# State space stage of a fused block: B held twice so that keys by queries is one product per batch, and another order of work in the first and the last group of heads

## The chip, the cores and the metric

The kernel runs on one core of a Trainium2 chip. The metric is the device time of one execution in microseconds (us); lower is better. The core's engines run side by side, each through its own list of instructions in a fixed order, and wait for one another on semaphores: TensorE (PE), which multiplies matrices, VectorE (DVE), ScalarE (ACT), GpSimd (POOL), and SyncE (SP), which here starts the transfers.

## What is computed

A block of three layers on x, 8 batches of 64 tokens with 512 features: cross attention over 1601 keys with 32 heads, then a Mamba-2 layer, then a routed mixture of rank 16 experts. The change is in the second. Cut to what matters:

```python
proj = x @ in_proj_w.T                       # gate | x, B, C | dt
xBC = silu(conv_bias + causal 4-tap conv of the x, B, C part)
dt = softplus(dt + dt_bias);  dA = exp(-dt * exp(A_log))
# 64 heads of 64 channels, 8 groups of 8 heads; a group shares B and C (128 each)
state = state * dA_t + (dt_t * x_t) outer B_t         # for each token t
y_t   = state @ C_t + D * x_t
y     = rmsnorm over a group's 512 channels * norm_weight * silu(gate)
out   = y @ out_proj_w.T
```

A scan over 64 tokens is done as a quadratic form: `y = (mask * exp(decays) * (B . C)) @ (dt * x)` for each batch and head.

## The kernel before

The stage `state_space_and_experts` loops over the 8 groups `g` of heads (0 to 7; `L` is 7), and within a group over 4 tiles `t` of 128 tokens (two batches each). A group takes ten **input chunks** of 128 columns of the input projection: `n` from 0 to 3 are the gates, 4 to 9 are four of x, then B, then C. `input_chunk(g, n)` is 12 f16 products of 128x128 by 128x512 into one of three banks `pI`, so that each chunk waits until the one three places before has been read. Its readers are, for a gate, `gates` on ACT, and for the rest `first_tap` (ACT), `taps` (three instructions on DVE) and `finish_conv` (ACT, which applies silu).

For a tile then come, on PE: `turn_x` (four transposes of x), `keys_by_queries` (B times C, f32), `decay` (sums of logarithms, from ramps that POOL makes with `ramp`), `outputs` (16 small products), `squares` (a sum for the norm) and `out_tile` (the output projection of one tile, again 12 products). On ACT `exponentials` reads what `decay` made, and `square` and `high` make squares and the f16 high half of y. On DVE `times_dt` multiplies the turned x by dt, `causal` masks keys by queries, `masked` joins them to the exponentials, `skip_added` and `gated` finish y, `accumulate` adds an output tile to x1, and `split_A`, `split_B` and `split_C` make f16 low halves of weights that arrived in f32 (A: the columns of x, B, C; B: the gates'; C: the output's). POOL has `ramp`, `join_squares`, `low` (the f16 low half of y) and `power` (the norm's root). After tile `t` of the last group the experts' work follows: `moments`, `normed`, `turn_normed`, `logits`, `route`, `turn_weighted`, `expert_out`, `add_experts`.

The order of all these calls is written out by hand, one list for each engine: `body` for groups 0 to 6, which interleaves a group with what is left of the one before, and `last` for group 7. In `body` a call `on(f, g, lag, ...)` is the call for group `g - lag`, and is left out where there is none. Tiles that share a PSUM bank are guarded by counts: `turn_x` waits until every `decay` begun so far has been read by its exponential,

```python
def turn_x(g, t):
    wait(pe, silu, CONV * g + GCH)
    wait(pe, dx, TT * g + t)
    wait(pe, e_ok, begun["d"])
```

and `out_tile` waits, as long as it uses the one bank `pO`, for the `accumulate` of the tile before. Ahead of the loop DVE computes dt for all groups in a chain of small instructions (L2005 to L2022). The first group's weights are loaded and split by `SsmStart`, during the attention's output projection.

## Time and profile before

| | |
|---|---|
| three runs | 2360.22, 2360.7, 2362.95 us (median 2360.7) |
| the profiled execution | 2363.03 us, span 2360.7 us |
| attention and its projections | to about 1938 us of the span |
| state space stage and experts | from about 1938 us to the end |
| mean granted clock of PE | 0.989 |

All durations below come from the one profiled execution. A row of a timeline gives start, duration, engine, line, operation, output from inputs, shape and count, and in brackets how long the engine had been idle and what released it. A product in f32 leaves two records, and records overlap, so that the time which a call takes on PE is read from its start to the start of the next. A granted clock of 1.00 is 2.4 GHz, 0.50 is 1.2 GHz.

### The profile page before, as it was taken

To read this page: it belongs to the slowest core of one execution; us is meant where nothing else is said; L and a number is where in the kernel's file an instruction comes from. 1 tells how busy PE (TensorE), PEld (TensorE's weight loads), DVE (VectorE), ACT (ScalarE), POOL (GpSimd) and SP (SyncE) were. 2 spreads that over 40 slices of the span, in tenths; PEclk is the share of its full clock that TensorE was granted. 3 is DMA by queue.
4 is the path that set the end of the run, shared out by engine and by line. 5 is a ranking of instruction groups with operands and counts; after the bars stand their busy time and mean duration, and the time that the engine had idled before them with its cause. 6 is when DMAs were issued, how large, how long until landed. Compare 5 with 4: busy or idle time off the path is not lost. (4 is left out here: it accounts for less than half of the span.)

```text
span 2360.7 us, 46502 instructions
## 1 busy us (share of the span) xinstructions
PE 2291.3 (97%) x19276; PEld 1651.5 (70%) x19276; DVE 1915.2 (81%) x2596; ACT 1295.4 (55%) x2085; POOL 1567.5 (66%) x1056
## 2 busy tenths in 40 slices
PE   7999999999999999999999999999999788999998
PEld 4567787788777887778877887778877344445544
DVE  6858888888888888888888888888879756888877
ACT  7845455554555455554555545554455336666664
POOL 0138888888888888888878888888878202334432
PEclk9999999999999999999999999999999998999999
DMA  8420000000001010010001000000002541212210
GB/s 287 125 53 28 26 26 26 29 26 26 26 26 32 19 34 26 18 28 26 26 26 32 27 26 26 26 28 10 11 26 63 166 164 48 98 64 81 90 46 19
DMA packets 101166, 117.54 MB, mean 50 GB/s; under 512 B 8286, under 2 KB 70878, under 8 KB 100958
## 3 DMA queue, kind: packets, MB, share of 16 engines
q1 hardware_dynamic: 98942, 107.25, 14.4%
q0 software_dynamic: 2016, 7.34, 1.2%
q8 instruction: 153, 2.51, 0.4%
q14 instruction: 55, 0.45, 0.1%
HBM read 96.74 MB, written 17.83 MB: 49 GB/s over the span
## 5 line engine op out<-in xcount | busy, mean ns | idle before, releaser
L174 POOL TENSOR_TENSOR p_l<-S,p_h 128x1792 f16<-128x1792 f32 x126 | 422.7, 3355 | 211.7 <-ACT p_h L469 211.7
L577 DVE SCALAR_TENSOR_TENSOR S<-pS,rk,mask 128x256 f32<-128x256 f32 x832 | 355.4, 477 | 133.0 <-PE pS L257 92.4
L257 PE MATMUL p_acc<-w_h,ctx_h 128*128 128x256 f16 (+1 forms) x1664 | 454.3, 273 | 0.0
L257 PE MATMUL p_acc<-w_l,ctx_h 128*128 128x256 f16 (+1 forms) x1664 | 454.3, 273 | 0.0
L257 PE MATMUL p_acc<-w_h,ctx_l 128*128 128x256 f16 (+1 forms) x1664 | 454.3, 273 | 0.0
L587 DVE TENSOR_REDUCE mx<-S 128x256 f32<-128x3328 f32 x64 | 382.7, 5980 | 2.2
L257 PE MATMUL p_acc<-ctx_h,w_h 128*128 128x400 f16 (+1 forms) x1024 | 341.3, 333 | 3.0 <-PEq L820 3.0
L257 PE MATMUL p_acc<-ctx_l,w_h 128*128 128x400 f16 (+1 forms) x1024 | 341.2, 333 | 0.0
L257 PE MATMUL p_acc<-ctx_h,w_l 128*128 128x400 f16 (+1 forms) x1024 | 340.4, 332 | 0.0
L451 ACT ACTIVATE v_h<-p_acc 128x512 f16<-128x512 f32 (+1 forms) x224 | 126.8, 566 | 379.5 <-PE p_acc L257 379.5
L679 POOL TENSOR_TENSOR sq_l<-sq_f,sq_h 128x400 f16<-128x400 f32 (+1 forms) x256 | 243.0, 949 | 69.9 <-ACT sq_h L443 69.9
L599 DVE TENSOR_TENSOR S<-S,pO 128x1792 f32<-128x1792 f32 (+1 forms) x128 | 240.2, 1878 | 6.8 <-PE pO L327 6.8
L257 PE MATMUL pO<-p_h,v_h 128*128 128x256 f16 x832 | 226.8, 273 | 3.1 <-DVE p_l L174 3.1
L257 PE MATMUL pS<-qh,k_h 128*128 128x256 f16 x832 | 226.5, 272 | 1.0 <-DVE S L577 1.0
L257 PE MATMUL pS<-qh,k_l 128*128 128x256 f16 x832 | 226.8, 273 | 0.0
L257 PE MATMUL pO<-p_h,v_l 128*128 128x256 f16 x832 | 226.8, 273 | 0.0
L257 PE MATMUL pO<-p_l,v_h 128*128 128x256 f16 x832 | 226.8, 273 | 0.0
L257 PE MATMUL pS<-ql,k_h 128*128 128x256 f16 x832 | 226.7, 272 | 0.0
L462 ACT ACTIVATE S<-S,lnb 128x1792 f32<-128x1792 f32 (+1 forms) x128 | 215.5, 1684 | 17.5 <-DVE S L599 17.5
L182 POOL TENSOR_TENSOR S<-S 128x1536 f32<-128x1536 f32 x63 | 216.8, 3441 | 0.1
L439 ACT ACTIVATE k_h<-p_acc 128x400 f16<-128x400 f32 (+1 forms) x256 | 129.8, 507 | 147.1 <-PE p_acc L257 145.1
L469 ACT ACTIVATE p_h<-S 128x1792 f16<-128x1792 f32 (+1 forms) x128 | 203.6, 1591 | 0.3
(286 smaller groups left out, 5229.9 us busy)
## 6 DMA issues: line engine op xcount, KB each, us to landing
ctx_p<-ctxT_dram SPq DMA_DIRECT2D x42, 458.0 KB, 3.5
s_wst<-winG_dram SPq DMA_DIRECT2D x8, 1536.0 KB, 6.4
q_wst<-wqT_dram SPq DMA_DIRECT2D x8, 1024.0 KB, 6.5
o_scratch<-o_st SPq DMA_DIRECT2D x32, 256.0 KB, 2.4
s_wst<-winG_dram SPq DMA_DIRECT2D x8, 1024.0 KB, 5.3
m_wost<-woutG_dram SPq DMA_DIRECT2D x8, 1024.0 KB, 5.3
qh<-q_hi_scratch SPq DMA_DIRECT2D x64, 64.0 KB, 1.9
ql<-q_lo_scratch SPq DMA_DIRECT2D x64, 64.0 KB, 2.0
```

The source lines that it names most:

```text
L174: eng.tensor_tensor(p_l[:, s % 2, t0:t1, :], S[:, s % 2, t0:t1, :], p_h[:, s % 2, t0:t1, :], ALU.subtract).then_inc(pl_ok, 1)
L182: eng.tensor_tensor(T[:, 0:6, :], T[:, 0:6, :], T[:, 6:12, :], ALU.add).then_inc(sum_ok, 1)
L257: mm = pe.matmul(out, x, y, start=first and j == 0, stop=final and j == 2)
L439: act.activation(k_h[:, head % 2, c0:c0 + w], bank[:, 0:w], ACT.Copy, scale=S_KV / (S_CTX * S_W))
L451: act.activation(v_h[0:m, job % 2, 2 * f:2 * f + tiles, :], pF[at % 3][0:m, 0:256 * tiles].rearrange("p (t c) -> p t c", c=256), ACT.Copy, ...
L462: act.activation(S[:, s % 2, t0:t1, :], S[:, s % 2, t0:t1, :], ACT.Exp, bias=lnb[:, 0:1]).then_inc(ph_ok, 1)
L469: act.activation(p_h[:, s % 2, t0:t1, :], S[:, s % 2, t0:t1, :], ACT.Copy).then_inc(ph_ok, 1)
L577: ins = dve.scalar_tensor_tensor(out=S[:, s % 2, t, :].rearrange("p (r q) -> p r q", r=REP), in0=bank[:, t % 2, :].rearrange("p (r q) -> p ...
L587: dve.tensor_reduce(mx[:, :], S[:, s % 2, :, :].rearrange("p t q -> p q t"), AX.X, ALU.max).then_inc(mx_ok, 1)
L599: dve.tensor_tensor(v, v, pO[s % 2][:, 1, :].unsqueeze(1).to_broadcast([P, t1 - t0, QC]), ALU.subtract).then_inc(sub_ok, 1)
L679: pool.tensor_tensor(sq_l[:, c0:c0 + w], sq_f[:, c0:c0 + w], sq_h[:, c0:c0 + w], ALU.subtract).then_inc(sql_ok, 1)
```

## The change

- `keys_by_queries` had, per batch of a tile, two products of 64 keys by 64 queries with the same operands, one for each half of the partitions of `pCB`. B is now held twice in `bq` (per batch, its 64 tokens and the same again), and one product of 128 by 64 writes both halves. `finish_conv` for B writes both copies, in one activation that reads its input twice.
- Groups 0 and 7 take the chunks in the order 4 to 9, 0 to 3. `place(g, n)` is a chunk's place among all, `order(g)` a group's order; banks and waits follow from them. The other groups keep 0 to 9.
- In group 0 all ten chunks, and ACT's work on them, are written as one run at the head of `body`, with `decay(0, 0)` behind them. `step_sizes` and the exponential of that `decay` come after the gates.
- `SsmStart` loads and splits A ahead of B. `split_B` of the next group waits for the place of the last gate chunk.
- `last` is written anew on PE, ACT, DVE and POOL.

```diff
     def load(self, sp, w):
+        sp.dma_start(self.wst[:, :, 0:CW], w[:, 0:CW].rearrange("(k p) c -> p k c", p=P)).then_inc(self.wA_in, 16)
         sp.dma_start(self.wst[:, :, CW:], w[:, CW:].rearrange("(k p) c -> p k c", p=P)).then_inc(self.wB_in, 16)
-        sp.dma_start(self.wst[:, :, 0:CW], w[:, 0:CW].rearrange("(k p) c -> p k c", p=P)).then_inc(self.wA_in, 16)
...
-        bc = sb("m_bc", [P, 2, ND])
+
+        bq = sb("m_bq", [P, BATCH, 2, TOK])
+        cq = sb("m_cq", [P, ND])
...
+        def order(g):
+
+            return (*range(GCH, NIN), *range(GCH)) if g in (0, L) else tuple(range(NIN))
+
+        def place(g, n):
+
+            return NIN * g + order(g).index(n)
...
                 if n == 0:
                     wait(pe, wB_lo, g + 1)
-                    wait(pe, conv, CONV * g)
                 if n == GCH:
                     wait(pe, wA_lo, g + 1)
-                if n >= 3 + GCH:
-                    wait(pe, conv, CONV * g + n - GCH - 2)
-                elif n >= 3:
-                    wait(pe, gat, GCH * g + n - 2)
+                m = place(g, n)
+                if m >= 3:
+
+                    og = (m - 3) // NIN
+                    on_ = order(og)[(m - 3) % NIN]
+                    if on_ < GCH:
+                        wait(pe, gat, GCH * og + on_ + 1)
+                    else:
+                        wait(pe, conv, CONV * og + on_ - GCH + 1)
...
                     cols = slice(t * P + 64 * b, t * P + 64 * b + 64)
-                    for e in range(2):
-                        mm = pe.matmul(pCB[64 * e:64 * e + 64, 64 * b:64 * b + 64], bc[:, 0, cols], bc[:, 1, cols], start=True, stop=True)
+                    mm = pe.matmul(pCB[:, 64 * b:64 * b + 64], bq[:, 2 * t + b, :, :].rearrange("p e q -> p (e q)"), cq[:, cols], start=True, stop=True)
                 mm.then_inc(cb, 1)
...
                 wait(act, wB_in, 16 * (g + 1))
-                wait(act, ip, NIN * (g - 1) + GCH)
+                wait(act, ip, place(g - 1, GCH - 1) + 1)
...
+                elif j == GCH:
+                    act.activation(bq[:, :, :, :], cv[:, j % 2, :].rearrange("p (b q) -> p b q", b=BATCH).unsqueeze(2).to_broadcast([P, BATCH, 2, TOK]),
+                                   ACT.Silu).then_inc(silu, 1)
                 else:
-                    act.activation(bc[:, j - GCH, :], cv[:, j % 2, :], ACT.Silu).then_inc(silu, 1)
+                    act.activation(cq[:, :], cv[:, j % 2, :], ACT.Silu).then_inc(silu, 1)
```

What the new lists do is seen from the instructions. First ACT in group 0, before (`m_gate` gates, `m_Ec` exponentials, `m_cv` first taps, `m_xq` silu of x, `m_dtq` step sizes):

```order
L1801 ACT_TABLE_LOAD
L1801 ACTIVATE m_gate<-m_b 128x512 x4
L1824 ACT_TABLE_LOAD
L1824 ACTIVATE m_Ec<-m_ab 128x512
L1808 ACTIVATE m_cv<-m_b,m_par 128x512 x2
L1816 ACT_TABLE_LOAD
L1816 ACTIVATE m_xq<-m_cv 128x8x64
L1808 ACTIVATE m_cv<-m_b,m_par 128x512
L1816 ACTIVATE m_xq<-m_cv 128x8x64
L1772 ACTIVATE m_dtq<-m_dt 64x128 x4
```

and the same group's end in the change (`m_bq` silu of B, twice as wide, `m_cq` of C, `s_wh` the next group's weights):

```order
L1846 ACTIVATE m_cv<-m_b,m_par 128x512
L1856 ACTIVATE m_bq<-m_cv 128x1024
L1859 ACTIVATE m_cq<-m_cv 128x512
L1839 ACTIVATE m_gate<-m_b 128x512 x4
L1810 ACTIVATE m_dtq<-m_dt 64x128 x4
L1865 ACT_TABLE_LOAD
L1865 ACTIVATE m_Ec<-m_ab 128x512
L1826 ACTIVATE s_wh<-s_wst 128x4x512
```

The first exponential has moved from behind the gates at the head to behind the gates at the end and the step sizes.

Second, DVE at the head of the last turn, before (`x` is `accumulate`, `m_yt` `skip_added`, `m_E` `masked`, `s_wl` the splits, B's with 512 and A's with 768 columns):

```order
L1985 SCALAR_TENSOR_TENSOR s_wl<-s_wst,s_wh 128x4x512
L2095 SCALAR_TENSOR_TENSOR x<-m_b,m_rs,x 128x512
L2068 SCALAR_TENSOR_TENSOR m_yt<-m_xq,m_par,m_cd 128x128 x4
L2059 TENSOR_TENSOR m_E<-m_Ec,m_cbm 128x512
L2078 TENSOR_TENSOR m_y<-m_yt,m_gate 128x512
L2051 TENSOR_TENSOR m_cbm<-m_cd,m_upto 128x128
L2059 TENSOR_TENSOR m_E<-m_Ec,m_cbm 128x512
L2068 SCALAR_TENSOR_TENSOR m_yt<-m_xq,m_par,m_cd 128x128 x4
L2078 TENSOR_TENSOR m_y<-m_yt,m_gate 128x512
L2095 SCALAR_TENSOR_TENSOR x<-m_b,m_rs,x 128x512
L2051 TENSOR_TENSOR m_cbm<-m_cd,m_upto 128x128
L1978 SCALAR_TENSOR_TENSOR s_wl<-s_wst,s_wh 128x4x768
```

and in the change:

```order
L2061 SCALAR_TENSOR_TENSOR s_wl<-s_wst,s_wh 128x4x512
L2135 TENSOR_TENSOR m_E<-m_Ec,m_cbm 128x512
L2171 SCALAR_TENSOR_TENSOR x<-m_b,m_rs,x 128x512
L2144 SCALAR_TENSOR_TENSOR m_yt<-m_xq,m_par,m_cd 128x128 x4
L2054 SCALAR_TENSOR_TENSOR s_wl<-s_wst,s_wh 128x4x768
L2127 TENSOR_TENSOR m_cbm<-m_cd,m_upto 128x128
L2171 SCALAR_TENSOR_TENSOR x<-m_b,m_rs,x 128x512
```

A's split has moved ahead of the second `accumulate`, that of tile 2 of group 5.

Third, PE late in the last turn, around the first `out_tile` of group 7, before (`L738` are chunks and output tiles, `L1610` keys by queries, `L1568` `decay`, `L1618` `squares`, `L1585` `outputs`, `L1599` `turn_x`):

```order
L1610 MATMUL m_cd<-m_bc 64x64 x4
L1568 MATMUL m_ab<-m_R,s_after 64x256 x4
L1610 MATMUL m_cd<-m_bc 64x64 x4
L1618 MATMUL m_cd<-s_ones,m_sqb 128x1
L1610 MATMUL m_cd<-m_bc 64x64 x4
L1585 MATMUL m_cd<-m_E,m_dtx 64x64 x16
L1568 MATMUL m_ab<-m_R,s_after 64x256 x4
L1599 MATMUL m_ab<-s_ident,m_xq 128x128 x4
```

and the same place in the change, with the last gate chunk ahead of it (12 rows of L738 each where the dots are, a chunk and then the output tile):

```order
L1624 MATMUL m_cd<-m_cq,m_bq 128x64 x2
...
L1632 MATMUL m_cd<-s_ones,m_sqb 128x1
L1624 MATMUL m_cd<-m_cq,m_bq 128x64 x2
L1583 MATMUL m_ab<-m_R,s_after 64x256 x4
L1600 MATMUL m_cd<-m_E,m_dtx 64x64 x32
...
L1624 MATMUL m_cd<-m_cq,m_bq 128x64 x2
L1614 MATMUL m_ab<-s_ident,m_xq 128x128 x4
```

Two tiles' `outputs` stand together now, and the keys of the last tile have moved behind the output tile. The whole new list of PE from there on: `out_tile(7,0)`, keys and `turn_x` of tile 3, `squares(7,1)`, `out_tile(7,1)`, `outputs(7,3)`, `turn_normed(0)`, `squares(7,2)`, `out_tile(7,2)`, `squares(7,3)`, `turn_normed(1)`, `logits(0)`, `logits(1)`, `out_tile(7,3)`. At its head the last turn has on PE: `out_tile(5,3)`, `decay(6,3)`, `outputs(6,2)`, `turn_x(6,3)`, chunk 4, keys of (6,3), `decay(7,0)`, chunk 5, `decay(7,1)`. Chunks 0 to 3 stand behind `out_tile(6,1)`, `turn_x(7,1)`, `turn_x(7,2)` and keys of (7,1).

## Rows read from the trace of the kernel before

**Rows 1.** Page, part 1: busy time of each engine and its share.

```profile
PE 2291.3 (97%) x19276; PEld 1651.5 (70%) x19276; DVE 1915.2 (81%) x2596; ACT 1295.4 (55%) x2085; POOL 1567.5 (66%) x1056
```

**Rows 2.** Busy time by stretch, middle: stretch, length, PE, PEld, DVE, ACT, POOL, PEclk, DMA.

```profile
2060.00:2120.00 60.00, 59.08 (x454) 30.17 (x452) 50.75 (x79) 40.44 (x53) 23.17 (x22) 1.00 0.22 74
```

**Rows 3.** Chain that ended last, two groups' first taps of C: start, us, what.

```profile
2071.18 0.79 ACT m_cv L1808
...
2117.83 0.79 ACT m_cv L1808
```

**Rows 4.** Busy time by stretch, both ends, columns as in rows 2.

```profile
1979.19:1993.05 13.86, 7.96 (x118) 5.51 (x116) 10.78 (x18) 10.44 (x11) 3.89 (x3) 0.69 0.24 76
2272.17:2343.98 71.81, 64.97 (x543) 33.41 (x537) 54.50 (x100) 35.99 (x54) 31.63 (x34) 0.95 0.07 24
2343.98:2360.70 16.72, 11.93 (x62) 6.82 (x59) 11.23 (x34) 3.38 (x9) 0.32 (x1) 0.98 0.17 63
```

**Rows 5.** Timeline of PE, middle: squares (L1618), keys (L1610), a chunk's first product.

```profile
2070.98 0.50 PE L1618 MATMUL m_cd<-s_ones,m_sqb 128*128 128x1 f32 x4
...
2097.59 0.28 PE L1618 MATMUL m_cd<-s_ones,m_sqb 128*128 128x1 f32 x2
2097.80 0.45 PE L1610 MATMUL m_cd<-m_bc 128*64 128x64 f32 x8
2098.18 0.39 PE L738 MATMUL m_b<-m_th,s_wh 128*128 128x512 f16 x1
...
2252.22 0.28 PE L1618 MATMUL m_cd<-s_ones,m_sqb 128*128 128x1 f32 x2
2252.36 0.38 PE L738 MATMUL m_b<-m_th,s_wh 128*128 128x512 f16 x1
```

**Rows 6.** Timeline of PE, from group 0 to group 1: keys, decay, next group's first chunk.

```profile
1983.19 0.45 PE L1610 MATMUL m_cd<-m_bc 128*64 128x64 f32 x8 [3.40 <-ACT m_bc L1818]
...
1985.11 1.13 PE L1568 MATMUL m_ab<-m_R,s_after 64*64 64x256 f32 x8 [0.42 <-DVE m_dtx L2044]
...
1993.05 0.61 PE L738 MATMUL m_b<-m_th,s_wh 128*128 128x512 f16 x1
```

**Rows 7.** Timeline of DVE, start of the stage: x1, end of the dt chain, first taps.

```profile
1935.51 2.49 DVE L1228 SCALAR_TENSOR_TENSOR x<-p_acc,p_x 128x512 f32<-128x512 f32 x4 [10.57 <-PE p_acc L738]
...
1960.67 0.29 DVE L2022 TENSOR_SCALAR m_dt<-m_dt 128x256 f32<-128x256 f32 x1
1967.25 2.27 DVE L2034 SCALAR_TENSOR_TENSOR m_cv<-m_b,m_par,m_cv 128x504 f32<-128x504 f32 x3 [6.29 <-ACT m_cv L1808]
```

**Rows 8.** Timeline of ACT, group 0: step sizes, weight split, table load, exponential.

```profile
1973.04 1.29 ACT L1772 ACTIVATE m_dtq<-m_dt 64x128 f32<-64x128 f32 x4
...
1983.05 1.89 ACT L1788 ACTIVATE s_wh<-s_wst 128x2048 f16<-128x2048 f32 x1
1984.96 1.28 ACT L1824 ACT_TABLE_LOAD   x1
1986.30 0.60 ACT L1824 ACTIVATE m_Ec<-m_ab 128x512 f32<-128x512 f32 x1
```

**Rows 9.** Busy time by stretch, after group 0's chunks, columns as in rows 2.

```profile
1985.00:1987.00 2.00, 1.14 (x9) 0.37 (x10) 2.00 (x3) 1.95 (x3) 0.66 (x1) 0.50 0.00 0
```

**Rows 10.** Timeline of PE, last turn: `turn_x(7,0)` and `decay(7,3)` after waits.

```profile
2309.86 0.63 PE L1599 MATMUL m_ab<-s_ident,m_xq 128*128 128x128 f32 x4 [2.16 <-ACT m_Ec L1824]
...
2325.44 0.90 PE L1568 MATMUL m_ab<-m_R,s_after 64*64 64x256 f32 x8 [1.39 <-POOL m_R L1444]
```

**Rows 11.** Chain that ended last, first and last `out_tile` of group 7.

```profile
2328.21 4.80 PE m_b L738 x12
...
2344.14 2.59 PE m_b L738 x12
```

**Rows 12.** Timeline of DVE, A's split in group 1 and in group 7.

```profile
1998.86 4.20 DVE L1978 SCALAR_TENSOR_TENSOR s_wl<-s_wst,s_wh 128x3072 f16<-128x3072 f32 x1
...
2275.63 3.34 DVE L1978 SCALAR_TENSOR_TENSOR s_wl<-s_wst,s_wh 128x3072 f16<-128x3072 f32 x1
```

More of the change, by code:

```diff
@@ L1552, in out_tile @@
                     wait(pe, conv, CONV * (g + 1))
+                    wait(pe, gat, GCH * (g + 1))
                 for j in range(GCH):
@@ L1702, in last @@
+                decay(g, 0)
+                input_chunk(g, 5)
+                decay(g, 1)
+                squares(g - 1, 0)
+                input_chunk(g, 6)
+                squares(g - 1, 1)
                 outputs(g - 1, 3)
-                input_chunk(g, 5)
+                input_chunk(g, 7)
                 out_tile(g - 1, 1 - par, 0)
-                input_chunk(g, 6)
                 squares(g - 1, 2)
-                input_chunk(g, 7)
                 input_chunk(g, 8)
+                squares(g - 1, 3)
@@ L1709, in last @@
                 input_chunk(g, 9)
-                squares(g - 1, 3)
-                decay(g, 0)
+                out_tile(g - 1, 1 - par, 1)
+                input_chunk(g, 0)
                 turn_x(g, 0)
-                out_tile(g - 1, 1 - par, 1)
+                out_tile(g - 1, 1 - par, 2)
+                turn_x(g, 1)
+                input_chunk(g, 1)
                 keys_by_queries(g, 0)
-                turn_x(g, 1)
-                out_tile(g - 1, 1 - par, 2)
-                decay(g, 1)
+                out_tile(g - 1, 1 - par, 3)
@@ L1718, in last @@
                 outputs(g, 0)
-                out_tile(g - 1, 1 - par, 3)
+                turn_x(g, 2)
+                input_chunk(g, 2)
+                decay(g, 2)
                 keys_by_queries(g, 1)
-                decay(g, 2)
+                input_chunk(g, 3)
+                squares(g, 0)
                 keys_by_queries(g, 2)
-                squares(g, 0)
+                decay(g, 3)
+                outputs(g, 1)
+                outputs(g, 2)
+                out_tile(g, par, 0, out_bank[0])
@@ L1724, in last @@
                 keys_by_queries(g, 3)
-                outputs(g, 1)
-                decay(g, 3)
-                turn_x(g, 2)
-                out_tile(g, par, 0, out_bank[0])
                 turn_x(g, 3)
-                outputs(g, 2)
+                squares(g, 1)
                 out_tile(g, par, 1, out_bank[1])
                 outputs(g, 3)
-                squares(g, 1)
+                turn_normed(0)
+                squares(g, 2)
                 out_tile(g, par, 2, out_bank[2])
-                squares(g, 2)
@@ L1797, in gates @@
             def gates(g, par, n):
-                wait(act, ip, NIN * g + n + 1)
+                wait(act, ip, place(g, n) + 1)
                 if n == 0:
                     wait(act, yg, TT * (g - 1))
-                act.activation(gate[:, par, n, :], pI[n % 3][:, :], ACT.Silu, scale=1.0 / (S_H * S_W)).then_inc(gat, 1)
+                act.activation(gate[:, par, n, :], pI[place(g, n) % 3][:, :], ACT.Silu, scale=1.0 / (S_H * S_W)).then_inc(gat, 1)
             def first_tap(g, j):
-                wait(act, ip, NIN * g + GCH + j + 1)
+                wait(act, ip, place(g, GCH + j) + 1)
                 wait(act, silu, CONV * g + j - 1)
@@ L2169, in last @@
                 split_B(g)
+                masked(g - 1, 1)
                 accumulate(g - 2, 1)
                 skip_added(g - 1, 0)
-                masked(g - 1, 1)
+                split_A(g)
+                causal(g - 1, 2)
+                accumulate(g - 2, 2)
+                times_dt(g - 1, 2)
+                skip_added(g - 1, 1)
+                masked(g - 1, 2)
                 gated(g - 1, 1 - par, 0)
-                causal(g - 1, 2)
-                masked(g - 1, 2)
-                skip_added(g - 1, 1)
@@ L2177, in last @@
                 gated(g - 1, 1 - par, 1)
-                accumulate(g - 2, 2)
+                skip_added(g - 1, 2)
+                times_dt(g - 1, 3)
+                accumulate(g - 2, 3)
                 causal(g - 1, 3)
-                split_A(g)
-                times_dt(g - 1, 2)
-                skip_added(g - 1, 2)
+                masked(g - 1, 3)
+                taps(g, 0)
                 split_C(g - 1, 1 - par)
-                masked(g - 1, 3)
-                times_dt(g - 1, 3)
+                skip_added(g - 1, 3)
@@ L2186, in last @@
+                taps(g, 1)
                 gated(g - 1, 1 - par, 2)
-                accumulate(g - 2, 3)
-                taps(g, 0)
-                skip_added(g - 1, 3)
+                taps(g, 2)
+                mean_square(g - 1)
                 gated(g - 1, 1 - par, 3)
-                taps(g, 1)
-                taps(g, 2)
+                accumulate(g - 1, 0)
                 taps(g, 3)
                 taps(g, 4)
-                mean_square(g - 1)
-                accumulate(g - 1, 0)
+                accumulate(g - 1, 1)
@@ L2219, in last @@
                 gated(g, par, 2)
-                times_dt(g, 3)
-                accumulate(g, 0)
-                skip_added(g, 3)
-                moments(0)
-                tile_mean_square(g, 1)
-                gated(g, par, 3)
+                accumulate(g, 0)
+                moments(0)
+                causal(g, 3)
+                masked(g, 3)
+                tile_mean_square(g, 1)
+                times_dt(g, 3)
                 normed(0)
                 accumulate(g, 1)
+                skip_added(g, 3)
@@ L2241, in last @@
                 route(2)
+                route(3)
                 add_experts(1)
-                route(3)
                 add_experts(2)
```

266 lines of the change are left out of this document (157 added, 109 removed).

## The prediction

> **What bounds the kernel now.** I read the page's head first, then busy time by stretch, the chain that ended last, and the timelines of the two places that the change touches. TensorE (PE) is busy for 97% of the span [rows 1]. The change leaves attention alone, so what counts is the state space stage, from 1940 us on. Its middle is bound by PE: in a 60 us stretch PE is busy 59.08 us at full clock, the vector engine (DVE) 50.75 [rows 2], and a group of heads comes every 46.65 us (2117.83 less 2071.18 [rows 3]). Its two ends are not. The first group has 13.86 us between its last input chunk and the next group's first, in which PE works 7.96 us at a mean clock of 0.69. In the last turn PE is idle 6.84 of the 71.81 us up to its last `out_tile`, and then 4.79 of 16.72 [rows 4]. So the middle can gain only by less PE work, the ends by shorter chains of waits.
>
> **Keys by queries, 32 calls.** Four products of 64x64 become two of 128x64, with the batch's B, held twice, as the 128 stationary columns. A call takes 0.38 us now, start to start (2097.80 to 2098.18 [rows 5]), for eight records. Half the records does not mean half the time. The row to go by is the one for squares: f32 as well, with 128 stationary columns and one moving column, and two more of its records cost 0.22 us (four are busy 0.50, two 0.28), so 0.11 each though almost nothing streams: the weights take that. Four such records make 0.44. On the other side, a call now also delays its neighbour: squares, keys and the next chunk take 0.59 (2097.59 to 2098.18), squares alone 0.14 (2252.22 to 2252.36), so keys really cost 0.45. Thus 0.45 now against 0.44 then: nothing. After a wait the first weights cannot be hidden, which costs up to 0.1 once per group; a call followed by a transpose may gain that. I take 0. Bounds: if a merged record kept the pace of one of today's records, a call would take 0.19, and 0.19 x 3 x 8 groups = 4.6 us go; the fourth call of a group stands before a `decay` that waits anyway. If each call grew by 0.06 (0.44 against 0.38), 1.4 us come.
>
> The Trainium skill, "TensorEngine Tiling (Array Packing)", sections Key Properties and Performance Considerations, speaks against the merger: products in different column tiles run in parallel, so merging two of them saves no streaming, though it saves the drain at a mode switch. The same section has the opposite rule too: a product with one moving column takes as long as one with 60, about 60 cycles, which here would make the call cheap. "TensorE: Matmul & The Clock Gate", section LDWEIGHTS, counts by stationary columns, P/1.2 ns: 107 ns for 128, and 0.43 for a call. The 0.11 of [rows 5] agrees with that.
>
> The copy of B makes one activation per group write 1024 elements per partition, not 512. The weight split writes 2048 in 1.89 us and the exponential 512 in 0.60 [rows 8], so, in line between them, about 1.03, 0.43 more. It runs while DVE does the 2.27 us of taps for C, which C's own activation awaits [rows 7, 8]: no cost in the middle. The other engines' middle order is as before.
>
> **First group.** Now gates go first, x, B, C last. The ten chunks end at 1979.19, where the first stretch of [rows 4] begins. A chunk takes 2.59, as an `out_tile` does [rows 11], and the one `decay` among them some 0.6, so counted back the fourth chunk starts at 1979.19 - 7 x 2.59 - 0.6 = 1960.5. The load order costs nothing either way: DVE sat idle for 10.57 us before 1935.51 with both splits behind it [rows 7].
>
> With x first, the fourth chunk needs the bank of the first, so the three taps of the first x chunk. DVE does its step-size chain until 1960.96 (1960.67 plus 0.29 [rows 7]), which the gates hid. The taps then end at 1960.96 + 2.27 = 1963.3, and only then can the fourth chunk start: 2.8 us of idle PE. Taps (2.27) keep ahead of chunks (2.59) afterwards, so the ten end at 1963.3 + 7 x 2.59 = 1981.5.
>
> Then what is late? `turn_x` of tile 0 waits until every begun `decay` has been read by its exponential. That `decay` now comes after the tenth chunk, and its exponential stands on ACT behind gate 3, four step-size copies (1.29) and a table load (1.28): 1981.65 + 0.60 + 1.29 + 1.28 + 0.60 = 1985.4 [rows 8]. So `turn_x` starts at 1985.4 and keys at 1985.9, where keys now start at 1983.19, after waiting 3.40 for C's activation [rows 6]. The transposed x must then still be multiplied by dt before the second transpose (0.68 and hops), so the second `decay` comes 2.35 us after keys, not 1.92 (1985.11 [rows 6]): 1988.25. From there to the next group's first chunk the order is the old one, 7.94 us (1993.05 less 1985.11 [rows 6]), if the clock falls as it did. Sum: 1996.2 against 1993.05, **3.1 us later**. Now, after 3.40 us of idle, the granted clock stands at 0.50 from 1985 on, the 1.2 GHz level [rows 9]. The new idle, 1982.1 to 1985.4, is as long. Were the clock not to fall, the 7.94 would shrink by about 2.2 (some 4.4 of the 7.96 busy us of this stretch [rows 4] run at half speed), and the loss is 0.9.
>
> **Last turn.** Now its chunks are gates first, and its end has short calls that wait for one another, without large ones between. After gaps of 2.16 and, with smaller ones about it, 1.39 [rows 10] `out_tile(7,0)` runs at half clock: some 4.8 us, where the last one takes 2.59 [rows 11]. With a `decay` and a transpose beside it the clock costs 3.0 us. With the gates last, chunks 0 to 3 lie between the last group's transposes, keys and outputs. I followed the new order by hand on all engines, each call with the duration that the trace has for it, from the state at 2264 on. Waits that I find:
> - At its start. `out_tile(5,3)` is first, and needs `accumulate(5,2)`, which on DVE now stands behind the A split (3.34 at best, 4.20 beside POOL's work [rows 12]). The split can start at 2269.1, when `skip_added(6,0)` is done, so accumulate ends at 2269.1 + 4.2 + 0.3 + 0.7 = 2274.3, where PE is ready at 2272.2: 2.1 us of new idle.
> - `outputs(7,2)` waits for `skip_added(7,1)`, behind `gated(7,0)` and `masked(7,2)` on DVE; the first of these needs gate 3, which on ACT stands behind two table loads (1.28 each [rows 8]): PE idle from 2322.9 to 2324.95, 2.05 us.
> - `squares(7,2)` still waits for `skip_added(7,3)`: 1.3 us.
> - Small ones: 0.3.
>
> Together 5.75 against 6.84 before [rows 4]. The work: 64.97 busy, less 3.0 for the clock, plus 1.5 for one transpose and `logits(1)` (1.03) that now come ahead of the last `out_tile`, is 63.5 [rows 4]. That puts the last `out_tile` at 69.2 after 2272.17, where it was at 71.81: 2.6 earlier. My walk from call to call, in which work eats part of the waits, puts it at 2339.4, 4.6 earlier. I take 3.6. Behind it, `route(1)` (some 1.3 us of small DVE steps) no longer stands between the last `accumulate` and its LayerNorm: 1.4 less. **5.0 us earlier.**
>
> **Sum.** 0 + 3.1 - 5.0 = -1.9 us on a profiled span of 2360.7. The profiled execution itself took 2363.03, 2.33 above its span and at the top of the runs shown (2360.22 to 2362.95, median 2360.7). Against the median: **2358.8 us**. A difference under 0.2% (4.7 us: 2356.0 to 2365.4) can hardly be told from none.
>
> **Rivals.**
> - *Both ends go well* (0.20): the clock stays up in the first group (loss 0.9) and the walk of the last turn holds (4.6 + 1.4 = 6.0): -5.1, 2355.6, down to 2353. For it: the walk has no step missing that I know. Against: 3.4 us of idle made the clock fall before.
> - *The merged product is cheap* (0.08): -4.6 more, 2354.2, down to 2351 with the first. The overhead rule of the tiling page is this one. The squares row speaks against it.
> - *The start costs more, slower* (0.10): the 2.8 us stall at 1960.5 makes the clock fall in the middle of dense chunks. A gap of 2.16 did not do it [rows 10], one of 3.40 did. Half speed over two or three chunks costs 2.6 each: 3.1 + 6.5 = 9.6 for the start, less 5.0: 2365.3. It decides where the start loses more than 9.7 us.
> - *The last turn gives little* (0.15): its new idle of 2.05 us lets the clock fall as before and the 3.0 stay: -1.9 + 3.0 = +1.1, 2361.8. Within 0.2%.
> - *Forecast* (0.47): 2355.9 to 2361.
>
> Faster by over 0.2%: the first two, 0.28. Slower by over 0.2%: the third, 0.10. Same: 0.62. The range takes in the rivals but for their outermost parts: 2352 to 2365. A gain beyond 8.7 us needs the first two at once.
>
> **What would show it.** In the new profile: keys with four records of about 0.11; a group still every 46.65 us (45.9 if the merger pays); PE idle near 1960.5 for 2.8 us before the fourth chunk, behind DVE taps; `turn_x` at about 1985.4, released by ACT's exponential; the second group's first chunk near 1996, with the clock at 0.50 before it; a 2 us wait at the start of the last turn for `accumulate`; no fall of the clock in its end; and the last `out_tile` about 16 us before the end. I am wrong if the first group is not later, if the middle moves, or if the clock falls elsewhere.

## The result and the profile after

The changed kernel takes 2364.57 us (median of 20 executions, 2362.18 to 2367.56) where the kernel before, measured beside it, takes 2361.53 (20 executions, 2359.72 to 2364.72): a ratio of 1.0014, with a 95% interval of 1.0008 to 1.0020. It is slower by 3.0 us, less than the 0.2% set as the bound for "no change", but on the other side of it than the 1.9 us of gain that were forecast. The profiled execution has a span of 2363.4 us, 2.7 more than before.

Page of the changed kernel, busy time (answers to [rows 1]):

```profile
PE 2295.2 (97%) x19148; PEld 1658.4 (70%) x19148; DVE 1913.6 (81%) x2596; ACT 1296.1 (55%) x2083; POOL 1569.0 (66%) x1056
```

TensorE has 128 instructions less (the 32 calls of keys by queries) and is yet busy 3.9 us longer. Of these 3.5 us lie in group 0, from its first chunk to the next group's (39.07 us busy, where it was 35.61): no added work, but work at a lower clock, as the next two views show. Busy time by stretch (stretch, length, PE, PEld, DVE, ACT, POOL, PEclk, DMA): the stall in group 0, the end of group 0, the middle, the last turn up to its last `out_tile`, and behind it. The last four answer to [rows 2, 4].

```profile
1959.00:1968.00 9.00, 5.78 (x20) 2.11 (x18) 7.43 (x12) 2.85 (x5) 2.04 (x2) 0.81 0.00 1
1982.76:1998.48 15.72, 10.19 (x114) 7.66 (x113) 8.04 (x14) 10.74 (x14) 4.89 (x4) 0.64 0.21 67
2060.00:2120.00 60.00, 59.19 (x467) 30.71 (x467) 50.75 (x81) 41.89 (x55) 21.94 (x21) 1.00 0.23 80
2276.54:2348.35 71.81, 66.98 (x573) 36.98 (x572) 54.73 (x107) 38.71 (x58) 27.31 (x31) 0.98 0.07 23
2348.35:2363.39 15.04, 10.59 (x50) 5.54 (x47) 9.60 (x30) 2.38 (x7) 0.55 (x1) 0.97 0.19 71
```

The middle is nearly as before. In the last turn PE is idle 4.83 of the 71.81 us, where it was idle 6.84, and the part behind the last `out_tile` is 15.04 us long and not 16.72. Both ends of group 0 run below full clock. PE there, in order of time (start, us, engine, line, what, and in brackets the idle time before and its releaser):

```profile
1950.66 0.61 PE L738 MATMUL m_b<-m_th,s_wh 128*128 128x512 f16 x1
...
1962.93 0.41 PE L738 MATMUL m_b<-m_th,s_wh 128*128 128x512 f16 x1 [3.22 <-DVE m_cv L2110]
1963.16 0.61 PE L738 MATMUL m_b<-m_tl,s_wh 128*128 128x512 f16 x1
...
1967.22 0.38 PE L738 MATMUL m_b<-m_th,s_wh 128*128 128x512 f16 x1
...
1982.85 0.66 PE L1583 MATMUL m_ab<-m_R,s_after 64*64 64x256 f32 x8
1986.75 0.81 PE L1614 MATMUL m_ab<-s_ident,m_xq 128*128 128x128 f32 x4 [3.24 <-issue]
...
1990.34 1.13 PE L1583 MATMUL m_ab<-m_R,s_after 64*64 64x256 f32 x8
...
1995.54 1.09 PE L1624 MATMUL m_cd<-m_cq,m_bq 128*128 128x64 f32 x4 [1.33 <-DVE m_yt L2144]
```

The fourth chunk waits 3.22 us for DVE's taps, and its 12 products then take 4.29 us (1962.93 to 1967.22) and not 2.59. `turn_x` starts 3.9 us after the start of the `decay` ahead of it. Its releaser reads "issue"; ACT at the same time shows what was late:

```profile
1982.96 0.60 ACT L1839 ACTIVATE m_gate<-m_b 128x512 f32<-128x512 f32 x1 [1.99 <-PE m_b L738]
1983.45 1.29 ACT L1810 ACTIVATE m_dtq<-m_dt 64x128 f32<-64x128 f32 x4
1984.76 1.28 ACT L1865 ACT_TABLE_LOAD   x1
1986.05 0.60 ACT L1865 ACTIVATE m_Ec<-m_ab 128x512 f32<-128x512 f32 x1
```

The exponential ends at 1986.65 and `turn_x` starts 0.1 later. The waits of the last turn on PE (the first one is that of `out_tile(5,2)`, the second that of `outputs(6,1)`):

```profile
2274.74 0.38 PE L738 MATMUL m_b<-m_woh,m_yh 128*128 128x512 f16 x1 [0.71 <-DVE x L2171]
...
2279.62 0.69 PE L1600 MATMUL m_cd<-m_E,m_dtx 64*64 64x64 f32 x32 [1.29 <-DVE m_cbm L2127]
...
2332.01 1.14 PE L1600 MATMUL m_cd<-m_E,m_dtx 64*64 64x64 f32 x32 [1.49 <-issue]
...
2343.06 0.35 PE L1632 MATMUL m_cd<-s_ones,m_sqb 128*128 128x1 f32 x2 [1.08 <-issue]
```

Keys by queries of tile 0 at two groups of before and, below, of the changed kernel:

```profile
2074.99 0.45 PE L1610 MATMUL m_cd<-m_bc 128*64 128x64 f32 x8 [0.41 <-ACT m_bc L1818]
...
2261.54 0.45 PE L1610 MATMUL m_cd<-m_bc 128*64 128x64 f32 x8 [0.41 <-ACT m_bc L1818]
```

```profile
2080.81 0.66 PE L1624 MATMUL m_cd<-m_cq,m_bq 128*128 128x64 f32 x4 [0.41 <-ACT m_cq L1859]
...
2267.64 0.66 PE L1624 MATMUL m_cd<-m_cq,m_bq 128*128 128x64 f32 x4 [0.41 <-ACT m_cq L1859]
```

With such rows the time can be laid out. From the first chunk to the next group's first chunk (1998.48 here): 47.82 us where it was 41.51 (1951.54 to 1993.05), **6.3 more**. From there to the keys of group 6: 269.16 where it was 268.49, **0.7 more**. From there to the end of the span: 95.76 where it was 99.16, **3.4 less**. Together 3.6 more; the stage begins 0.9 us earlier, by attention's scatter, and 2.7 remain in the span.

### The profile page after: what moved, and what is told of

Same layout as the page of the kernel before. It is cut to its first block and busy times, and to the rows that moved or that the text cites. A ratio compares the mean times of both kernels' runs of the same rounds, so it can differ in the third digit from the quotient of the medians.

```text
span 2363.4 us, 46244 instructions
## 1 busy us (share of the span) xinstructions
PE 2295.2 (97%) x19148; PEld 1658.4 (70%) x19148; DVE 1913.6 (81%) x2596; ACT 1296.1 (55%) x2083; POOL 1569.0 (66%) x1056
```

## Experiments

Each round was timed beside the kernel before, on the same chip; the rounds ran on three chips. Ratios are to the kernel before in the same round; they are not the quotients of the medians. One thing helps to read the profiles: the first chunk of the stage starts between 1948.71 and 1953.61 us in the fourteen profiled executions, by the scatter of attention, so whole spans are compared less well than lengths within the stage.

**The parts one by one.** Four kernels: the changed one with group 0 in its old order (all three edits of group 0 undone: chunks, ACT's list, the load order), and the kernel before with one part each.

Without the new start:

```diff
-            return (*range(GCH, NIN), *range(GCH)) if g in (0, L) else tuple(range(NIN))
+            return (*range(GCH, NIN), *range(GCH)) if g == L else tuple(range(NIN))
```

> The change without its new first group: group 0 in the old order on TensorE and ScalarE, B's weights loaded first, the rest as changed. Theory (the first group lost what the last turn won): in the two profiles the stretch from the first chunk to group 1's first chunk grew from 41.5 to 47.8 us, so this one is 6.3 us faster than the change and some 3 us faster than the kernel before (ratio 0.9988). Rival (the merged keys or the last turn lost the time, the first group is even): no faster than the kernel before, 1.0010 or more.

Merged keys alone:

```diff
-                    for e in range(2):
-                        mm = pe.matmul(pCB[64 * e:64 * e + 64, 64 * b:64 * b + 64], bc[:, 0, cols], bc[:, 1, cols], start=True, stop=True)
+                    mm = pe.matmul(pCB[:, 64 * b:64 * b + 64], bq[:, 2 * t + b, :, :].rearrange("p e q -> p (e q)"), cq[:, cols], start=True, stop=True)
```

> The kernel before with the merged keys by queries alone (B held twice, one product per batch). Theory: four records 0.112 us apart cost what eight did, a group's period goes from 46.64 to 46.71 us, +0.5 us over the run, a ratio of 1.0000 to 1.0005. Rival (a merged product is cheap, each call 0.19 less): -4.6 us, 0.998. Rival (the merger is what cost the time): +3 us, 1.0013.

The new last turn alone (`last` of PE, ACT, DVE and POOL as in the change):

```diff
-            return tuple(range(NIN))
+            return (*range(GCH, NIN), *range(GCH)) if g == L else tuple(range(NIN))
```

> The kernel before with the new last turn alone (its order on four engines, x, B, C ahead of the gates in group 7; keys and group 0 as before). Theory: -3.4 to -4 us, a ratio of 0.9983 to 0.9986. Rival (the last turn gives nothing by itself, the apparent gain belongs to a slower start that gave it slack): within 1 us of the kernel before, 0.9996 or more.

The new start alone (`body` of PE and ACT and `SsmStart` as in the change):

```diff
-            return tuple(range(NIN))
+            return (*range(GCH, NIN), *range(GCH)) if g == 0 else tuple(range(NIN))
```

> The kernel before with the new first group alone (chunks x, B, C, gates in one run, A's weights first). Theory: group 1's first chunk comes 6.3 us later after the first chunk of group 0, and all of it reaches the end: +6.3 us, 1.0027. Forecast of the prediction for this part: +3.1 us, 1.0013. Rival (the middle absorbs it): under +1.5 us.

| | median, us | ratio | 95% |
|---|---|---|---|
| without the new start | 2359.00 | 0.9987 | 0.9978 to 0.9996 |
| merged keys alone | 2364.08 | 1.0004 | 0.9995 to 1.0013 |
| new last turn alone | 2358.79 | 0.9985 | 0.9976 to 0.9994 |
| new start alone | 2368.45 | 1.0026 | 1.0015 to 1.0036 |

The kernel before took 2361.86 us in this round. The parts add up: 0.0004 + 0.0026 - 0.0015 is 0.0015, and the whole measured 0.0014 (each part is known to about 0.001). The new start costs 6.1 us, and that alone turns a gain of 3 us into a loss. The traces say the same: from the first chunk to the end of the span it takes 409.2 us before, 415.7 with the new start alone, 405.3 with the new last turn alone, 404.8 without the new start and 412.7 in the changed kernel.

The merged keys alone need a closer look. Their executions lie in two groups, five from 2361.18 to 2361.87 us and six from 2364.08 to 2365.35. The profiled one is of the slower group, and in its last turn, which has the old order, the clock fell behind the wait before `turn_x(7,0)`:

```profile
2309.91 0.63 PE L1614 MATMUL m_ab<-s_ident,m_xq 128*128 128x128 f32 x4 [2.16 <-ACT m_Ec L1841]
2310.37 0.38 PE L738 MATMUL m_b<-m_woh,m_yh 128*128 128x512 f16 x1
...
2314.65 0.56 PE L1624 MATMUL m_cd<-m_cq,m_bq 128*128 128x64 f32 x4
```

The output tile behind it takes 4.28 us (2310.37 to 2314.65). In the kernel before the same wait of 2.16 us [rows 10] is followed by an output tile of 2.68 us (2310.32 to 2313.00). That this fall is what parts the two groups of executions is likely and not shown; nor is it shown whether the merged keys have a part in it.

**The first wait of the new start, filled.** The changed kernel with 14 products that nobody reads, in the place where PE stands idle:

```diff
                     on(input_chunk, g, 0, 6)
+                    for _ in range(14):
+                        pe.matmul(pO[:, :], wh[:, 0, 0:P], th[:, 0, :], start=True, stop=True)
                     on(input_chunk, g, 0, 7)
```

> The changed kernel with 14 extra products (first tile of weights by tokens, 128x512 f16, into the bank that is free then) ahead of the fourth chunk of group 0; nothing reads them. In the changed kernel TensorE stands idle 3.2 us there and the fourth chunk then takes 4.29 us, where a chunk takes 2.59. Theory: the 1.7 us are the clock, which fell in the idle time. With the stall filled (14 x 0.216 = 3.0 us) the fourth chunk takes 2.6 us and everything behind it comes 1.7 us earlier: about 2362.9, 1.0006 of before where the change alone gave 1.0014. Rival: the fourth chunk is slow for a cause of its own (its bank, its weights, the taps beside it): it stays at 4.3 us and the time at 1.0014.

Measured: 2361.25 us, 0.9999 (0.9990 to 1.0008). PE in this kernel, and the stretch that is the first of the result's table:

```profile
1959.51 3.19 PE L1674 MATMUL m_b<-m_th,s_wh 128*128 128x512 f16 x14
1962.94 0.39 PE L738 MATMUL m_b<-m_th,s_wh 128*128 128x512 f16 x1 [0.24 <-DVE m_cv L2112]
...
1965.54 0.38 PE L738 MATMUL m_b<-m_th,s_wh 128*128 128x512 f16 x1
```

```profile
1959.00:1968.00 9.00, 8.76 (x42) 3.82 (x40) 8.15 (x14) 3.65 (x6) 2.04 (x2) 1.00 0.00 1
```

The fourth chunk starts at the same time as without them (1962.94, 1962.93) and takes 2.60 us, at a clock of 1.00: the 1.7 us were the clock. Group 0 takes 45.54 us (1950.67 to 1996.21) and not 47.82, 2.3 less. The other 0.6 us lie behind the chunks: the same wait of 3.24 us stands before `turn_x`, but here `turn_x` and the first keys behind it still run at full clock (0.63 and 0.56 us, where the changed kernel has 0.81 and 0.95), and it is three calls later that the clock is low. The ratios differ by 0.0015, 3.5 us, and their intervals meet at 1.0008. This execution also ran its last turn at full clock (below), which fits the rest, but one profile of each kernel doesn't show how their medians come about.

**The second wait of the new start, removed.** The first `decay` and its exponential come earlier:

```diff
                     on(input_chunk, g, 0, 9)
+                    on(decay, g, 0, 0)
                     on(input_chunk, g, 0, 0)
...
-                    on(decay, g, 0, 0)
...
                     on(gates, g, 0, par, 0)
+                    step_sizes()
+                    on(exponentials, g, 0, 0)
                     on(gates, g, 0, par, 1)
                     on(gates, g, 0, par, 2)
                     on(gates, g, 0, par, 3)
-                    step_sizes()
-                    on(exponentials, g, 0, 0)
```

> The changed kernel with the first decay on TensorE moved from behind the tenth chunk to behind C's, and on ACT the step sizes and its exponential moved between gates 0 and 1 (one more table load). Theory: turn_x of tile 0 waits 3.24 us for that exponential alone, so it now follows the last chunk at once. Gates 1 to 3, the next weight split and the second exponential come later on ACT, about 4.4 us behind keys where they were 3.1: gain 3.9 - 1.3 = 2.6 us, and up to 2 us more if the granted clock stays at 1.00 behind the chunks: 2360 to 2362, ratio 0.9995 to 1.0003. Rival: turn_x has another late input (the transposed x's step sizes, a silu) or the second exponential eats the gain: under 1 us gained, ratio above 1.001.

Measured: 2360.39 us, 0.9991 (0.9982 to 1.0000): the time is at the better end of the expectation, the ratio a little beyond it. PE:

```profile
1965.79 0.39 PE L738 MATMUL m_b<-m_th,s_wh 128*128 128x512 f16 x1 [3.16 <-DVE m_cv L2110]
...
1986.31 0.60 PE L1614 MATMUL m_ab<-s_ident,m_xq 128*128 128x128 f32 x4
1986.75 0.56 PE L1624 MATMUL m_cd<-m_cq,m_bq 128*128 128x64 f32 x4
...
1991.05 0.66 PE L1583 MATMUL m_ab<-m_R,s_after 64*64 64x256 f32 x8 [1.14 <-issue]
```

`turn_x` has no wait in front of it, and it, the keys and both `decay` run at full clock (0.66 us, where the changed kernel has 1.13). The clock falls only for the last calls, from 1993.51 on. Group 0 takes 42.93 us (1953.51 to 1996.44), 4.9 less than in the changed kernel. So the exponential behind the gates was all that `turn_x` waited for.

**Another order of group 0.** On the kernel before with the new last turn: two gates, x, B, C, two gates. On ACT the first exponential stands behind the third `first_tap` and the step sizes behind the fifth.

```diff
+            if g == 0:
+                return (0, 1, *range(GCH, NIN), 2, 3)
...
+                    input_chunk(0, 6)
+                    decay(0, 0)
+                    input_chunk(0, 7)
+                    input_chunk(0, 8)
+                    input_chunk(0, 9)
+                    turn_x(0, 0)
+                    input_chunk(0, 2)
+                    input_chunk(0, 3)
```

> The kernel before with the new last turn (0.9985, 2358.8) and group 0's chunks in the order 0, 1, 4 to 9, 2, 3: two gates ahead hide the step-size chain on DVE (no stall before the third or sixth chunk), two gates behind hide the taps and the silu of C. Theory: keys of tile 0 start when the chunks and turn_x are done, 1979.2 where they start at 1982.6 now: 3.4 us gained, less about 0.9 because the second exponential then stands behind the weight split on ACT, plus up to 2 us if the granted clock stays at 1.00 there: 2 to 5 us below the new last turn alone, ratio 0.9965 to 0.9977. Rival: the order of chunks only moves the wait, since the second exponential and the next group's weights bound the tail of group 0: under 1 us gained, ratio above 0.998.

Measured: 2355.32 us, 0.9972 (0.9962 to 0.9982). PE:

```profile
1979.89 0.45 PE L1626 MATMUL m_cd<-m_bc 128*64 128x64 f32 x8
...
1984.40 1.13 PE L1584 MATMUL m_ab<-m_R,s_after 64*64 64x256 f32 x8 [1.93 <-issue]
1985.28 1.11 PE L1601 MATMUL m_cd<-m_E,m_dtx 64*64 64x64 f32 x32
1987.71 0.69 PE L1626 MATMUL m_cd<-m_bc 128*64 128x64 f32 x8 [1.33 <-DVE m_yt L2143]
```

Neither the wait for DVE's chain nor that of 3.40 us for C's silu [rows 6] is left: the keys start without one. The ratio is in the middle of the expectation. In the trace the gain is at the small end of it, 2.1 us (group 0 takes 39.37 us, 1951.08 to 1990.45, where it took 41.51 before), since `decay(0,2)` now waits 1.93 us for the exponential before it, and the clock falls there.

**The head of the last turn.** On the kernel before with the new last turn: A's low half in two pieces of 384 columns, with a semaphore for the first.

```diff
                 skip_added(g - 1, 0)
-                split_A(g)
+                half_A(g, slice(0, CW // 2), wA_half)
                 causal(g - 1, 2)
...
                 masked(g - 1, 2)
+                half_A(g, slice(CW // 2, CW), wA_lo)
```

> The kernel before with the new last turn (0.9985), in which DVE makes A's low half for group 7 in two pieces: columns 0 to 383 where the split stands, columns 384 to 767 behind masked(6,2). Theory: outputs(6,1) waits 1.16 us at the head of the last turn because causal(6,2) stands behind the 3.62 us split on DVE. With a first piece of 1.8 us causal(6,2) follows its keys at once, that wait goes, and the last out_tile comes 1.2 us earlier: ratio 0.9980. Rival: the wait moves on to outputs(6,2), turn_x(6,3) or chunk 7, which waits for the second piece: no gain, 0.9985.

Measured: 2356.70 us, 0.9978 (0.9968 to 0.9988). `outputs(6,1)` follows its neighbours without a wait, where the changed kernel has 1.29 us:

```profile
2271.48 0.66 PE L1618 MATMUL m_ab<-s_ident,m_xq 128*128 128x128 f32 x4
2272.14 0.69 PE L1604 MATMUL m_cd<-m_E,m_dtx 64*64 64x64 f32 x32
```

The ratio's interval overlaps that of the new last turn alone, so the 1.2 us are shown by the trace and not by the ratios: from the keys of group 6 to the last `out_tile` it takes 78.0 us here and 79.1 with the mixed start, which has the same last turn without the pieces. The clock stayed up in both executions.

**Both, and the waits filled.** The mixed start with the two pieces; then with useless products in the two waits of group 0; then also ahead of `outputs(7,2)`.

```diff
+                if g == 0:
+                    for _ in range(8):
+                        pe.matmul(pO[0:SSM_HEADS, :], wdh[:, 0, :], th[:, 0, :], start=True, stop=True)
                 on(decay, g, 0, 2)
...
+                if g == 0:
+                    for _ in range(5):
+                        pe.matmul(pO[0:SSM_HEADS, :], wdh[:, 0, :], th[:, 0, :], start=True, stop=True)
                 on(keys_by_queries, g, 0, 2)
...
+                wait(pe, acc, TT * G)
+                for _ in range(5):
+                    pe.matmul(pO[0:SSM_HEADS, :], wdh[:, 0, :], th[:, 0, :], start=True, stop=True)
                 outputs(g, 2)
```

> Group 0 in the mixed order (two gates, x, B, C, two gates), the new last turn, and A's low half for group 7 in two pieces. Theory: the two edits touch stretches 300 us apart and add up: the mixed start gave 0.9972 with the new last turn, and the pieces are worth 1.2 us (the wait of outputs(6,1) that they removed): about 0.9967, 2354.3 where the kernel before takes 2362.2. Rival: what the pieces gained was only the clock, which stayed at full speed in the end of that execution's last turn; then nothing is added: 0.9972.

> The same with extra products of no use (64x512, f16, into a bank that is free) in two waits of group 0: 8 ahead of decay(0,2), which waits 1.93 us, and 5 ahead of keys(0,2), which waits 1.33 us. Theory: without them the granted clock falls to 0.50 from 1984 on and outputs, keys, turn_x and the next chunk's first products take 1.1, 0.69, 1.1, 1.1 and 0.61 us instead of 0.65, 0.45, 0.65, 0.65 and 0.38, about 2 us in all; with them it stays at 1.00 and the time falls by up to 2 us: 0.9959. Rival: the next group's first chunk then waits for its weights' low half, or the products delay what they stand ahead of: no gain, 0.9967.

> The same with 5 more such products ahead of outputs(7,2), which waits 1.46 us. In the new last turn that wait is followed by half clock in some executions (the changed kernel, the new last turn alone: 1.1 us for outputs and 3.8 for out_tile(7,0)) and not in others, with the same list of instructions. Theory: filled, the clock stays up in all of them, and the median falls by about half of the 1.7 us that a fall costs: 0.8 us, 0.9956. Rival: the clock of that place hangs on something else than that wait: no change of the median.

Measured: 2355.28 (0.9972, 0.9961 to 0.9983), 2351.91 (0.9957, 0.9943 to 0.9970) and 2350.18 (0.9951, 0.9937 to 0.9964). The pieces added nothing that can be measured to the mixed start: its rival's number came out. The two were timed in different rounds. The traces offer the clock as a reason: in the profiled execution with the pieces it fell in the last turn (0.89 and 0.77 in two stretches of 5 us), in that of the mixed start alone it did not. That this holds for the other executions isn't shown. Filling group 0's waits lowered the ratio by 0.0015, 3.5 us; every execution with them (2351.10 to 2353.73) is faster than every one without (2354.88 to 2355.90). The stretch that holds them, first without, then with the products:

```profile
1982.80:1989.20 6.40, 3.17 (x51) 2.63 (x52) 4.39 (x8) 5.56 (x5) 4.09 (x2) 0.62 0.43 139
```

```profile
1984.00:1990.50 6.50, 6.00 (x105) 3.51 (x97) 5.58 (x10) 6.17 (x7) 4.05 (x2) 1.00 0.39 124
```

Group 0 then takes 37.70 us (1952.89 to 1990.59), where it took 39.39 with the waits open (1951.36 to 1990.75): 1.7 us, near the 2 expected. In the two profiled executions another 1.6 us come from the last turn up to its last `out_tile`, which ran at full clock with the products and not without them. Whether that is also where the other 1.8 us between the medians lie, one profile of each cannot say. Whether the third filling adds something is not settled: 0.9951 against 0.9957, with intervals that overlap. In the two profiled executions, where the clock stayed up in the last turn with and without it, it adds nothing: from the first chunk to the end of the span it takes 398.5 us with it and 398.4 without.

**The price of a f32 product.** The merged keys with each product issued twice:

```diff
+                    for _ in range(2):
                         mm = pe.matmul(pCB[:, 64 * b:64 * b + 64], bq[:, 2 * t + b, :, :].rearrange("p e q -> p (e q)"), cq[:, cols], start=True, stop=True)
```

> The kernel before with keys by queries merged (1.0004), in which each of the merged products is issued twice with the same operands. Theory: a f32 product with 128 stationary columns costs two records of 0.112 us whatever streams through it, so a call grows by 4 records, 0.45 us, and 32 calls by 14.3 us, nearly all on the path: 1.0062. Rival: most of the 0.112 is the change between this call's form and its neighbours', paid once: the repeated product costs half or less, under 7 us, 1.003.

Measured: 2381.14 us, 1.0077 (1.0062 to 1.0093), 17 us over the merged keys alone, which were timed in another round. Keys of tile 0, four groups apart, with each merged product issued once (the merged keys alone) and twice:

```profile
2027.69 0.66 PE L1624 MATMUL m_cd<-m_cq,m_bq 128*128 128x64 f32 x4 [0.41 <-ACT m_cq L1835]
...
2214.53 0.66 PE L1624 MATMUL m_cd<-m_cq,m_bq 128*128 128x64 f32 x4 [0.42 <-ACT m_cq L1835]
```

```profile
2034.02 1.10 PE L1625 MATMUL m_cd<-m_cq,m_bq 128*128 128x64 f32 x8 [0.42 <-ACT m_cq L1836]
...
2228.67 1.10 PE L1625 MATMUL m_cd<-m_cq,m_bq 128*128 128x64 f32 x8 [0.41 <-ACT m_cq L1836]
```

A group takes 48.66 us and not 46.71: 1.95 for 16 more records, 0.12 each. Over 8 groups that is 15.6 us. The rival is out; 128 stationary columns in f32 cost about 0.12 us a record even with the same operands again.

## Why the prediction was wrong

**Keys merged: right.** Forecast 0. The group's period is 46.71 us (2080.81 to 2267.64, by 4) where it was 46.64, 0.07 more, and the part alone measured 1.0004 with 1 in its interval, though its executions lie in two groups (above). By the period, keys are some 0.4 of the 0.7 us that the middle grew, an estimate from 0.07 a group. The page "TensorE: Matmul & The Clock Gate" of the Trainium skill, section LDWEIGHTS, which prices weights by stationary columns (0.107 us for 128), agrees with what this kernel shows (0.11 a record by [rows 5], 0.12 by the doubled products). The overhead rule of "TensorEngine Tiling (Array Packing)" of the Trainium skill, section Performance Considerations, by which a product with few moving columns costs about 60 cycles, is not borne out here. The gain of 4.6 us, my price for a cheap merged product, did not come.

**First group: the step that failed.** Forecast 3.1 us, measured 6.3. Of the missing 3.2:
- 0.5: the taps start 9.94 us after the first chunk (1960.60), and I had put them at 9.42. Between the end of DVE's chain and the taps lie 0.5 us that I left out.
- 1.7: "the fourth chunk" runs at half clock for most of its length. I counted 2.8 us of idle time there and took the chunk behind it at 2.59. The filled stall shows the 1.7 us directly. In the sum this term stood at nothing. It was my rival "the start costs more", to which I gave 0.10 with two or three slow chunks; it is one chunk.
- 0.9: the tail. I took "the old order, 7.94 us, if the clock falls as it did". But before, `turn_x` and the first keys were done at full clock ahead of the fall (0.45 for keys at 1983.19 [rows 6]); now they stand behind the wait, and the clock is low from `turn_x` on (0.95 for the keys). Some 0.6 of this hangs on when the clock falls: with the stall filled it fell three calls later behind the same wait, and from `turn_x` to the next group's first chunk it took 11.13 us (1985.08 to 1996.21), not 11.73.

The remaining 0.1 is rounding: 1963.3 + 7 x 2.59 is 1981.4 and not 1981.5. What stands behind each wait was right: `turn_x` was forecast 3.9 us behind the last chunk's `decay` and came there.

**Last turn: right in its mechanism, its size hung on the clock.** Forecast -5.0, measured -3.4, of which -1.68 behind the last `out_tile` (forecast -1.4) and -1.72 ahead of it (forecast -3.6). The waits that I named are there: 0.71 and 1.29 at the head for "2.1 us of new idle" (neither at `out_tile(5,3)`: the first at `out_tile(5,2)`, whose `accumulate` stands on DVE behind B's split and a `masked`, the second at `outputs(6,1)`, which waits for a `causal` behind A's split), 1.49 for 2.05, 1.08 for 1.3, and 0.96 of small ones for 0.3: 5.5 for 5.75, of which 4.83 lie in the 71.81 us of the table. The step that failed is "less 3.0 for the clock": I had the clock stay up behind the wait before `outputs(7,2)`. Here it fell, but for shorter. The stretch of the wait and the one behind it, in the changed kernel, and in the one without the new start, which has the same list and the same wait (1.49):

```profile
2328.40:2333.40 5.00, 3.30 (x80) 2.39 (x79) 4.20 (x11) 3.86 (x7) 2.19 (x3) 0.84 0.00 0
2333.40:2338.40 5.00, 5.00 (x26) 2.73 (x25) 3.15 (x7) 2.90 (x5) 3.84 (x4) 0.82 0.01 3
```

```profile
2318.90:2323.90 5.00, 3.39 (x53) 2.11 (x51) 3.32 (x10) 3.85 (x5) 1.02 (x1) 1.00 0.00 0
2323.90:2328.90 5.00, 4.91 (x58) 3.19 (x59) 3.94 (x8) 4.37 (x8) 4.25 (x6) 1.00 0.02 3
```

The chain that ended last has `out_tile(7,0)` and the last one, here in the changed kernel:

```profile
2333.14 3.75 PE m_b L738 x12
...
2348.52 2.60 PE m_b L738 x12
```

and the last one in the kernel without the new start, with that kernel's keys of group 6 from its timeline of PE:

```profile
2339.02 2.60 PE m_b L738 x12
```

```profile
2259.62 0.66 PE L1624 MATMUL m_cd<-m_cq,m_bq 128*128 128x64 f32 x4 [0.42 <-ACT m_cq L1835]
```

From the keys of group 6 to the last `out_tile` it takes 79.40 us there, 80.88 in the changed kernel (2348.52 less 2267.64), and 82.60 before (2344.14 [rows 11] less 2261.54). With the clock up the new last turn is 3.2 us shorter ahead of the last `out_tile`, near the 3.6 forecast, and 1.5 us of it go when the clock falls. So the rival "the last turn gives little" was true in part, in this execution.

**The other rivals.** "Both ends go well" (0.20) needed the clock up in the first group, and it fell there in two places. Its loss of 0.9 was also reckoned from too little: in the trace of before not "some 4.4" but 5.8 busy us ran at 0.50 (from 1985 to 1993). "The merged product is cheap" (0.08) is out by the doubled products. The profile's signs that I had set were "the first group is not later, the middle moves, or the clock falls elsewhere": the last one came, at 1963 and at 2332.

**The sum.** 0.7 + 6.3 - 3.4 = 3.6 against 0 + 3.1 - 5.0. Two of my terms were wrong in the same direction and for the same reason: I knew that the clock falls behind a wait and asked, for each place, whether it would, from one gap of 2.16 and one of 3.40 us. One execution each was too little for that: behind the gap of 2.16, which "did not do it", the clock did fall in the profiled executions of the merged keys alone and of the doubled products. A new stall in the midst of dense chunks should have carried its 1.7 us in the sum and not only in a rival.

## What to carry to other kernels

A wait of TensorE costs twice where the clock falls with it: price it by its length and by the work behind it at 1.2 GHz, and put both in the sum. One execution in which the clock stayed up behind a wait is no proof that it will do so in the next. When a stage's first pass is reordered to shorten its end, look at what the old order hid at its beginning (here VectorE's chain of step sizes, behind the gates) and at what the moved work now stands behind on another engine (here an exponential behind gates, copies and a table load); an order that leaves both covers in place (gates at both ends) made group 0 2.1 us shorter, where the all-or-nothing order made it 6.3 longer. A wait of 2 us that cannot be removed may still be worth filling with products that nobody reads.

## What the hardware showed

- The same list of instructions with the same wait on PE has its clock fall behind the wait in some executions and not in others. Nine profiled executions have the new last turn with nothing filled in it, and a wait of 1.46 to 1.50 us before `outputs(7,2)`. The clock fell there in four (the changed kernel, the new last turn alone, the early `decay`, the mixed start with the pieces), with 1.5 us at stake, and stayed at 1.00 in five. Their last turns are of three kinds (keys merged, keys as before, keys as before with the pieces), and each kind is among both the four and the five. The old last turn shows it less cleanly: behind its wait of 2.16 us the clock stayed at 1.00 in the kernel before and with the new start alone, and fell in the merged keys alone (an output tile of 4.28 us and not 2.68) and in the doubled products (4.27), which both have the merged keys. Why is not settled; it wasn't tried to shift the wait alone. "TensorE: Matmul & The Clock Gate" of the Trainium skill, in its part on the clock gate, says that one kernel shows different numbers of slow products from run to run, by the phase of a window that runs freely; it says so of a kernel's start. These executions are in keeping with that, and don't show it.
- Products that nobody reads, put into waits of 3.22, 1.93 and 1.33 us, kept the granted clock at 1.00 behind them in every profiled execution. The fourth chunk behind 14 of them started at the same time as without (1962.94, 1962.93) and took 1.7 us less; the 13 in the other two waits together made group 0 1.7 us shorter.
- A f32 product with 128 stationary columns costs two records of 0.12 us also when it repeats the one before it.
- The fastest kernel measured (mixed start, two pieces, all three waits filled) takes 2350.18 us, 0.9951 of the kernel before; with nothing filled, 2355.28.
